# Self attention on one core: another order for VectorE's maxima and sums and for ScalarE's exponentials and copies

## The chip, the cores and the metric

The kernel runs on one core of a Trainium2 chip. The metric is the device time of one execution in microseconds (us). A core has five engines that run at the same time, each through its own list of instructions, in order: TensorE (PE in the profile; PEld is its weight loads), VectorE (DVE), ScalarE (ACT), GpSimd (POOL) and SyncE (SP). They wait for each other through semaphores only.

## The reference, cut to what matters

Three blocks with residuals over 32 batches of 128 tokens of width 128: causal self attention with 16 heads of 64, cross attention (16 heads of 8, with 128 context keys beside 128 own), and a mixture of 8 experts. The change is in the first:

```python
def self_attention(resid_stream, ...):            # called with layernorm(x): two norms in a row
    x = _layernorm(resid_stream, ln_w, ln_b)
    q = jnp.einsum('bsd,hde->bshe', x, W_q) + b_q        # k and v likewise
    scores = jnp.einsum('bqhe,bkhe->bhqk', q, k) * D_HEAD ** -0.5
    scores = jnp.where(causal, scores, -jnp.inf)
    pattern = jax.nn.softmax(scores, axis=-1)
    z = jnp.einsum('bhqk,bkhe->bqhe', pattern, v)
    return jnp.einsum('bqhe,hed->bqd', z, W_o) + b_o
x = x + self_attention(layernorm(x), ...)
```

## The kernel before

Self attention handles one batch b at a time, in four steps g = 0 to 3 (the loop over `steps`). The 16 heads of a batch are four *units* of four heads; a unit's scores (128 x 512) fill one PSUM bank. Scores for units 0 and 1 (banks 0 and 1) are one product group of TensorE in g = 0, those for units 2 and 3 (banks 2 and 3) one in g = 1. All engines run the same loop over b and g; each has its own function `self_attention` with its own order, and the order in it is written by hand. `valid(k)` says whether batch b + k exists; `back(b, parity, g, k, n)` gives the unit that was handled k steps earlier, which may be of the batch before.

For one unit the path is: scores (TensorE), `reduce_max` (VectorE, L638), four exponentials (ScalarE, L529), `reduce_sum` and `reciprocal` (VectorE, L644 and L647), multiply of the probabilities by the inverse sums (GpSimd, L388), four transposes (TensorE, L993) into bank 6, copy to `probsT` (ScalarE, L521). After unit 3 of a batch come the products with v (z, TensorE, in banks 0 and 1), two z copies (ScalarE, L539), the output product with `wo` and the residual (VectorE, L692).

Beside this run the projections for batch b + 1 (TensorE through banks 4 and 5: q in g = 0, k in g = 1, v in g = 2; VectorE copies q at L656 and k at L661, ScalarE copies v at L546), and the two norms of batch b + 2: statistics and aggregate (VectorE, L680 and L683) in g = 0 and again in g = 1, an rstd for each (GpSimd, L395 and L398), `zln` (L674) and `xn` (L686) on VectorE, the transpose of `xn` (TensorE, L950) and `xT` (VectorE, L633), which GpSimd splits in two float16 parts (L380 and L382).

TensorE's order in a batch b is:

- g = 0: scores of units 0 and 1; transposes of unit 2 of b - 1; q projection of b + 1
- g = 1: scores of units 2 and 3; transposes of unit 3 of b - 1; k projection
- g = 2: z of b - 1; transposes of unit 0 of b; v projection
- g = 3: transpose of xn of b + 2; transposes of unit 1 of b; output product of b - 1 (it waits for `sa_z_taken` and `sa_xT_taken`)

GpSimd's order is: g = 0: multiply of unit 3 of b - 1, first rstd of b + 2; g = 1: multiply of unit 0, second rstd; g = 2: multiply of unit 1; g = 3: split of xT, multiply of unit 2, bias to the residual.

In batches 30 and 31 (`run_joined`) the first steps of cross attention stand between the steps of self attention, and a last pass with b = 32 finishes batch 31. Then follow cross attention and the experts.

Of the kernel before, what the change touches and what calls it, by code (L numbers as in the profile page):

```python
# [20 lines left out]
ACT = mybir.ActivationFunctionType  # L21
AX_X = mybir.AxisListType.X

P = 128
# [5 lines left out]
G1 = 4  # L30
HPG = H // G1
E2 = D // H
HALVES = 2
# [64 lines left out]
def back(b, parity, g, k, n):  # L98

    off, unit = divmod(g - k, n)  # L100
    return off, unit, (parity + off) % 2


def build(nc, x, ctx, W_q, W_k, W_v, W_o, b_q, b_k, b_v, b_o, ln_w, ln_b, w_qkv, w_proj, b_proj,
          gate_w, gate_proj_w, up_proj_w, down_proj_w, out):
    es = ExitStack()
    with es:
        def sb(name, shape, dt=F32):
            return es.enter_context(nc.sbuf_tensor(name, shape, dt))

        def sem(name):
            return es.enter_context(nc.semaphore(name))
# [50 lines left out]
        probs = sb("probs", [P, 4, 512])  # L163
        probsT = sb("probsT", [P, 4, 512])
        zT = sb("zT", [P, PAIRS, P])
        nmax = sb("nmax", [P, 8, 4])
        rsum = sb("rsum", [P, 8, 4])
        rinv = sb("rinv", [P, 8, 4])
# [52 lines left out]
        ps = [es.enter_context(nc.psum_tensor(f"ps{i}", [P, 512], F32)) for i in range(8)]  # L221
# [28 lines left out]
        sa_scores = sem("sa_scores"); sa_max = sem("sa_max"); sa_exp = sem("sa_exp")  # L250
        sa_sums = sem("sa_sums"); sa_inverse_sums = sem("sa_inverse_sums")
# [40 lines left out]
        def bcast(ap, n):  # L292

            return ap.unsqueeze(2).to_broadcast([ap.shape[0], ap.shape[1], n])
# [208 lines left out]
        def _(act):  # L503
# [12 lines left out]
            def self_attention(b, parity, valid, steps):  # L516
                def copy_transposed(g):
                    off, u, _ = back(b, parity, g, 2, G1)
                    if valid(off):
                        act.wait_ge(sa_pT_in_bank, G1 * (b + off) + u + 1)  # L520
                        nc.scalar.copy(probsT[:, u, :], ps[6][:, :]).then_inc(sa_pT_taken, 1)  # L521

                for g in steps:
                    if g != 2:
                        copy_transposed(g)
                    if valid(0):
                        act.wait_ge(sa_max, G1 * b + g + 1)
                        for i in range(HPG):
                            last = nc.scalar.activation(probs[:, g, i * P:(i + 1) * P],  # L529
                                                        ps[g][:, i * P:(i + 1) * P], ACT.Exp,  # L530
                                                        bias=nmax[:, g, i:i + 1])
                        last.then_inc(sa_exp, 1)
                    if g == 2 and valid(-1):
                        n = b - 1
                        if valid(-2):
                            act.wait_ge(sa_output, n)
                        for half in range(HALVES):
                            act.wait_ge(sa_z_in_bank, HALVES * n + half + 1)
                            nc.scalar.copy(zT[:, 4 * half:4 * half + 4, :], ps[half][:, :]).then_inc(sa_z_taken, 1)  # L539
                    if g == 2:  # L540
                        copy_transposed(g)
                    if g == 2 and valid(1):
                        n, np_ = b + 1, (parity + 1) % 2
                        for half in range(2):
                            act.wait_ge(sa_projected, 6 * n + 5 + half)
                            nc.scalar.activation(v1[:, np_, 512 * half:512 * half + 512], ps[4 + half][:, :], ACT.Copy,  # L546
                                                 scale=1.0 / (X1_SCALE * W_SCALE)).then_inc(sa_v_taken, 1)
# [74 lines left out]
        def _(dve):  # L622
# [2 lines left out]
            dve.wait_ge(ln_ready, 1)  # L625

            def self_attention(b, parity, valid, steps):
                for g in steps:
                    if g == 3 and valid(2):
                        dve.wait_ge(sa_xT_in_bank, b + 3)  # L630
                        if valid(1):
                            dve.wait_ge(sa_x_low, b + 2)
                        nc.vector.tensor_scalar(xT[:, :], ps[7][:, 0:P], lnwb[:, 0:1], lnwb[:, 1:2],  # L633
                                                ALU.mult, ALU.add).then_inc(sa_xT_taken, 1)

                    if valid(0):
                        dve.wait_ge(sa_scores, HALVES * b + g // 2 + 1)
                        nc.vector.reduce_max(nmax[:, g, :], ps[g][:, :].rearrange("p (h k) -> p h k", h=HPG),  # L638
                                             AX_X, negate=True).then_inc(sa_max, 1)
                    off, u, _ = back(b, parity, g, 1, G1)  # L640
                    if valid(off):
                        t = G1 * (b + off) + u
                        dve.wait_ge(sa_exp, t + 1)
                        nc.vector.reduce_sum(rsum[:, u, :], probs[:, u, :].rearrange("p (h k) -> p h k", h=HPG),  # L644
                                             AX_X).then_inc(sa_sums, 1)
                        dve.wait_ge(sa_sums, t + 1)
                        nc.vector.reciprocal(rinv[:, u, :], rsum[:, u, :]).then_inc(sa_inverse_sums, 1)  # L647

                    if valid(1) and g < 2:
                        n, np_ = b + 1, (parity + 1) % 2  # L650
                        for half in range(2):
                            dve.wait_ge(sa_projected, 6 * n + 2 * g + half + 1)
                            tiles = ps[4 + half][:, :].rearrange("p (t q) -> p t q", t=4)
                            own = slice(4 * half, 4 * half + 4)
                            if g == 0:
                                last = nc.vector.scalar_tensor_tensor(  # L656
                                    out=qT[:, np_, own, :], in0=tiles,
                                    scalar=E1 ** -0.5 / (X1_SCALE * W_SCALE), in1=bcast(bq[:, own], P),
                                    op0=ALU.mult, op1=ALU.add)
                            else:  # L660
                                last = nc.vector.scalar_tensor_tensor(  # L661
                                    out=kT[:, np_, own, :], in0=tiles, scalar=1.0 / (X1_SCALE * W_SCALE),
                                    in1=bcast(bk[:, own], P), op0=ALU.mult, op1=ALU.add)
                            last.then_inc(sa_qk_taken, 1)

                    if valid(2):
                        n = b + 2
                        if g == 0:
                            if valid(-2) and not valid(-3):
                                dve.wait_ge(x_rest_loaded, 16)  # L670
                            src = x_all[:, n, :]
                        if g == 1:
                            dve.wait_ge(sa_rstd, 2 * n + 1)
                            nc.vector.tensor_scalar(zln[:, :], x_all[:, n, :], mv[:, 0, 0:1], rstd[:, 0:1],  # L674
                                                    ALU.subtract, ALU.mult).then_inc(sa_first_norm, 1)
                            dve.wait_ge(sa_first_norm, n + 1)
                            src = zln[:, :]
                        if g < 2:
                            dve.sem_inc(alone)
                            nc.vector.bn_stats(bst[:, g, :], src).then_inc(sa_stats, 1)  # L680
                            dve.wait_ge(sa_stats, 2 * n + g + 1)
                            dve.sem_inc(alone)
                            nc.vector.bn_aggr(mv[:, g, :], bst[:, g, :]).then_inc(sa_mean_var, 1)  # L683
                        if g == 2:
                            dve.wait_ge(sa_rstd, 2 * n + 2)
                            nc.vector.tensor_scalar(xn[:, :], zln[:, :], mv[:, 1, 0:1], rstd[:, 1:2],  # L686
                                                    ALU.subtract, ALU.mult).then_inc(sa_norm, 1)
                    if g == 3 and valid(-1):
                        n = b - 1
                        dve.wait_ge(sa_output, n + 1)  # L690
                        dve.wait_ge(sa_bias_added, n + 1)
                        nc.vector.tensor_tensor(x_all[:, n, :], ps[7][:, P:2 * P], x_all[:, n, :],  # L692
                                                ALU.add).then_inc(sa_residual, 1)
# [575 lines left out]
```

## Time and profile before

| | |
|---|---|
| time, three runs | median 1242.4 us (1242.32 to 1245.7) |
| profiled execution | 1243.03 us, span of the core 1241.3 us |
| TensorE busy | 1153.1 us, 93% of the span |
| VectorE busy | 943.1 us, 76% |
| ScalarE busy | 834.6 us, 67% |
| GpSimd busy | 453.6 us, 37% |
| self attention | from about 26 to 496 us of the span |

The span is what the trace shows of the core; the execution's time is a little longer. In the rows below times are in us from the start of the span; a row of a timeline is one instruction or several alike (xN), with its start and its duration, and in brackets how long the engine was idle before it and who released it. Matmul durations overlap, since matmuls are pipelined.

### The profile page before, as it was taken

How to read it: one execution, taken by the hardware profiler on the slowest of the kernel's cores; microseconds unless marked ns; L12 is line 12 of the kernel's file. 1: busy time of each engine (PE TensorE's matmuls, PEld its weight loads, DVE VectorE, ACT ScalarE, POOL GpSimd, SP SyncE). 2: the span in 40 equal slices, each digit the busy share in tenths (PEclk: the TensorE clock that was granted, in tenths of full speed). 3: DMA queues.
4: the chain of work that ended last, by engine and by line, in shares of the span. 5: the costliest groups of instructions: out<-in, count | busy, mean ns of one | idle time of the engine just before them, and what ended most of it. 6: DMA issues, size and time to landing. Idle time of an engine off the chain costs nothing.

```text
span 1241.3 us, 31536 instructions
## 1 busy us (share of the span) xinstructions
PE 1153.1 (93%) x11818; PEld 869.5 (70%) x11851; DVE 943.1 (76%) x2242; ACT 834.6 (67%) x2374; POOL 453.6 (37%) x796
## 2 busy tenths in 40 slices
PE   5889999998999997999999999999996899999997
PEld 4677777777777776777777777777774566656564
DVE  5876677776667774888888888888886778888887
ACT  2556555566555554888888888888885565555554
POOL 3544444444444443232323323233222332222222
PEclk9999999999999998999999999999998899999999
DMA  6000000000000000000000000000030000000000
GB/s 158 2 2 2 2 1 2 2 2 2 2 1 2 2 2 5 10 11 14 10 11 11 10 15 10 11 10 11 24 94 1 1 10 10 11 10 10 10 10 10
DMA packets 20666, 16.06 MB, mean 13 GB/s; under 512 B 7042, under 2 KB 18596, under 8 KB 20516
## 3 DMA queue, kind: packets, MB, share of 16 engines
q1 hardware_dynamic: 20176, 13.90, 4.1%
q8 instruction: 96, 1.57, 0.5%
q14 instruction: 54, 0.44, 0.1%
q10 hardware_dynamic: 340, 0.14, 0.1%
HBM read 11.94 MB, written 2.10 MB: 11 GB/s over the span
## 4 chain that ended last, share of the span: by engine, by line
PE 52%; issue 16%; ACT 16%; DVE 10%; POOL 6%; DMA 1%; SPq 0%; DVEq 0%; POOLq 0%
PE ps L942 38%; PE ps L1087 7%; ACT probs L564 5%; POOL h_lo L492 5%; PE ps L993 5%; DVE kT L661 3%; ACT probsT L555 3%; ACT zT L539 2%; ACT probs L529 2%; DVE nmax L638 2%; ACT probsT L521 1%; ACT k_hi L559 1%; DVE bst L680 1%; DMA wv<-in_L_attn_W_v 1%; PE ps L1120 1%
## 5 line engine op out<-in xcount | busy, mean ns | idle before, releaser
L564 ACT ACTIVATE probs<-ps,nmax 128x256 f32<-128x256 f32 x512 | 239.2, 478 | 11.2 <-DVE nmax L783 10.6
L783 DVE TENSOR_REDUCE nmax<-ps 128x2 f32<-128x512 f32 x256 | 176.3, 689 | 48.2 <-PE ps L942 45.0
L529 ACT ACTIVATE probs<-ps,nmax 128x128 f32<-128x128 f32 x512 | 148.4, 390 | 72.4 <-DVE nmax L638 72.4
L388 POOL TENSOR_TENSOR probs<-probs,rinv 128x512 f32<-128x512 f32 x128 | 133.4, 1042 | 147.2 <-DVE rinv L647 145.3
L521 ACT COPY probsT<-ps 128x512 f32<-128x512 f32 x128 | 78.4, 612 | 127.4 <-PE ps L993 127.4
L942 PE MATMUL ps<-probsT,vm 128*32 128x128 f32 x2048 | 161.5, 279 | 0.0
L555 ACT COPY probsT<-ps 128x512 f32<-128x512 f32 x224 | 131.9, 589 | 34.8 <-PE ps L1087 32.6
L1087 PE MATMUL ps<-ident,probs 128*128 128x128 f32 x1024 | 153.8, 273 | 1.2 <-ACT probs L564 1.1
L492 POOL TENSOR_TENSOR h_lo<-wk,h_hi 128x512 f16<-128x512 f32 x64 | 74.0, 1156 | 185.4 <-ACT h_hi L612 182.4
L604 ACT ACTIVATE wq<-ps 128x512 f32<-128x512 f32 x128 | 76.6, 598 | 73.2 <-PE ps L942 73.1
L1087 PEld LDWEIGHTS ps<-ident,probs 128*128 128x128 f32 x1024 | 119.6, 141 | 5.0 <-ACT probs L564 2.1
L942 PEld LDWEIGHTS ps<-probsT,vm 128*32 128x32 f32 x2048 | 92.8, 109 | 42.7 <-issue 42.6
L993 PE MATMUL ps<-ident,probs 128*128 128x128 f32 x512 | 83.6, 286 | 41.3 <-ACT probsT L521 37.1
L638 DVE TENSOR_REDUCE nmax<-ps 128x4 f32<-128x512 f32 x128 | 86.1, 672 | 38.5 <-PE ps L942 38.5
L564 ACT ACTIVATION_READ_ACCUMULATOR probs<-ps,nmax 128x1 f32 x512 | 105.8, 207 | 0.0
L612 ACT CAST h_hi<-wk 128x512 f16<-128x512 f32 x128 | 77.9, 617 | 40.9 <-DVE wk L921 40.8
L926 DVE TENSOR_TENSOR h_lo<-wk,h_hi 128x512 f16<-128x512 f32 x64 | 71.8, 1123 | 43.8 <-ACT h_hi L612 43.8
L942 PE MATMUL ps<-kT,qm 128*128 128x256 f16 x512 | 98.2, 274 | 5.7 <-ACT probs L564 5.4
L942 PE MATMUL ps<-xnT_hi,w_hi 128*128 128x512 f16 x256 | 99.6, 389 | 2.7 <-DVE wk L921 2.7
L942 PE MATMUL ps<-xnT_lo,w_hi 128*128 128x512 f16 x256 | 98.9, 386 | 0.0
L993 PEld LDWEIGHTS ps<-ident,probs 128*128 128x128 f32 x512 | 54.0, 141 | 63.8 <-POOL probs L388 50.7
L942 PE MATMUL ps<-xnT_hi,w_lo 128*128 128x512 f16 x256 | 98.6, 385 | 0.0
(194 smaller groups left out, 2872.3 us busy)
## 6 DMA issues: line engine op xcount, KB each, us to landing
ctx_row<-in_ctx SPq DMA_DIRECT2D x32, 128.0 KB, 2.0
out_x<-x_all SPq DMA_DIRECT2D x8, 256.0 KB, 2.3
kT<-in_L_ffn_down_proj_w SPq DMA_DIRECT2D x1, 1024.0 KB, 10.9
wq<-in_L_attn_W_q SPq DMA_DIRECT2D x1, 512.0 KB, 5.1
wk<-in_L_attn_W_k SPq DMA_DIRECT2D x1, 512.0 KB, 9.3
wv<-in_L_attn_W_v SPq DMA_DIRECT2D x1, 512.0 KB, 9.7
wo<-in_L_attn_W_o SPq DMA_DIRECT2D x2, 256.0 KB, 6.1
x_all<-in_x SPq DMA_DIRECT2D x1, 256.0 KB, 3.1
```

The costliest lines, as they stand in the source:

```text
L388: nc.gpsimd.tensor_tensor(pr, pr, bcast(rinv[:, u, :], P), ALU.mult).then_inc(sa_probs, 1)
L492: nc.gpsimd.tensor_tensor(h_lo[:, e % 2, 0, :], hT[:, 0, :], h_hi[:, e % 2, 0, :], ALU.subtract).then_inc(hidden_low_first, 1)
L521: nc.scalar.copy(probsT[:, u, :], ps[6][:, :]).then_inc(sa_pT_taken, 1)
L529: last = nc.scalar.activation(probs[:, g, i * P:(i + 1) * P], ps[g][:, i * P:(i + 1) * P], ACT.Exp, bias=nmax[:, g, i:i + 1])
L555: nc.scalar.copy(probsT[:, u % 4, :], ps[2 + u % 2][:, :]).then_inc(ca_pT_taken_act, 1)
L564: last = nc.scalar.activation(probs[:, g % 4, i * KEYS2:(i + 1) * KEYS2], ps[SCORE_BANKS2[g]][:, i * KEYS2:(i + 1) * KEYS2], ACT.Exp, bias ...
L612: nc.scalar.copy(h_hi[:, e % 2, i, :], hT[:, i, :]).then_inc(hidden_high, 1)
L638: nc.vector.reduce_max(nmax[:, g, :], ps[g][:, :].rearrange("p (h k) -> p h k", h=HPG), AX_X, negate=True).then_inc(sa_max, 1)
L783: nc.vector.reduce_max(nmax[:, g, 0:2], ps[SCORE_BANKS2[g]][:, :].rearrange("p (h k) -> p h k", h=2), AX_X, negate=True).then_inc(ca_max, 1)
L942: return nc.tensor.matmul(o, l, r, start=start, stop=stop, **kw)
L993: last = nc.tensor.transpose(ps[6][:, i * P:(i + 1) * P], probs[:, u, i * P:(i + 1) * P], ident[:, :])
L1087: last = nc.tensor.transpose(ps[2 + u % 2][:, i * P:(i + 1) * P], probs[:, u % 4, i * P:(i + 1) * P], ident[:, :])
```

## The change

VectorE takes the maxima of units 0 and 1 in g = 0 and does in g = 1: sum 0, maximum 2, sum 1, maximum 3. Sums 2 and 3 follow in g = 2 and 3 of the same batch (unit 3's was in g = 0 of the next). ScalarE does the exponentials of units 0 and 1 in g = 0, of unit 2 in g = 1, of unit 3 in g = 2 behind the z copies and the copy of transposed unit 0; the v copies go to g = 3, behind the copy of transposed unit 1. TensorE's, GpSimd's and SyncE's programs are unchanged, as is the number of instructions of each kind.

```diff
@@ ScalarE, self_attention @@
+                def exponentials(u):
+                    if valid(0):
+                        act.wait_ge(sa_max, G1 * b + u + 1)
+                        for i in range(HPG):
+                            last = nc.scalar.activation(probs[:, u, i * P:(i + 1) * P],
+                                                        ps[u][:, i * P:(i + 1) * P], ACT.Exp,
+                                                        bias=nmax[:, u, i:i + 1])
+                        last.then_inc(sa_exp, 1)
+
                 for g in steps:
-                    if g != 2:
-                        copy_transposed(g)
-                    if valid(0):
-                        act.wait_ge(sa_max, G1 * b + g + 1)
...
-                        last.then_inc(sa_exp, 1)
+                    if g == 0:
+                        copy_transposed(0)
+                        exponentials(0)
+                        exponentials(1)
+                    if g == 1:
+                        copy_transposed(1)
+                        exponentials(2)
                     if g == 2 and valid(-1):
...
                             nc.scalar.copy(zT[:, 4 * half:4 * half + 4, :], ps[half][:, :]).then_inc(sa_z_taken, 1)
                     if g == 2:
-                        copy_transposed(g)
-                    if g == 2 and valid(1):
+                        copy_transposed(2)
+                        exponentials(3)
+                    if g == 3:
+                        copy_transposed(3)
+                    if g == 3 and valid(1):
                         n, np_ = b + 1, (parity + 1) % 2
@@ VectorE, self_attention @@
+                def maximum(u):
+                    if valid(0):
+                        dve.wait_ge(sa_scores, HALVES * b + u // 2 + 1)
+                        nc.vector.reduce_max(nmax[:, u, :], ps[u][:, :].rearrange("p (h k) -> p h k", h=HPG),
+                                             AX_X, negate=True).then_inc(sa_max, 1)
+
+                def sums(off, u):
+                    if valid(off):
+                        t = G1 * (b + off) + u
+                        dve.wait_ge(sa_exp, t + 1)
+                        nc.vector.reduce_sum(rsum[:, u, :], probs[:, u, :].rearrange("p (h k) -> p h k", h=HPG),
+                                             AX_X).then_inc(sa_sums, 1)
+                        dve.wait_ge(sa_sums, t + 1)
+                        nc.vector.reciprocal(rinv[:, u, :], rsum[:, u, :]).then_inc(sa_inverse_sums, 1)
...
-                    if valid(0):
-                        dve.wait_ge(sa_scores, HALVES * b + g // 2 + 1)
...
-                    off, u, _ = back(b, parity, g, 1, G1)
-                    if valid(off):
...
+                    if g == 0:
+                        maximum(0)
+                        maximum(1)
+                    if g == 1:
+                        sums(0, 0)
+                        maximum(2)
+                        sums(0, 1)
+                        maximum(3)
+                    if g >= 2:
+                        sums(0, g)
```

## Rows read from the trace of the kernel before

**Rows 1.** Windows: busy us (instructions) of each engine, TensorE's clock, DMA.

```profile
53.18:455.81 402.63, 367.16 (x4296) 303.74 (x4324) 282.70 (x672) 233.66 (x672) 192.78 (x308) 1.00 0.01 2
469.71:496.41 26.70, 20.80 (x179) 17.74 (x178) 12.50 (x30) 10.77 (x28) 8.12 (x12) 0.81 0.02 6
485.00:488.00 3.00, 1.17 (x6) 0.84 (x8) 0.62 (x2) 0.22 (x2) 1.04 (x1) 0.66 0.00 0
```

**Rows 2.** Line L993 (transposes of probabilities): for whom TensorE sat idle.

```profile
  ACT probsT L521: 34.8, 29
```

**Rows 3.** Timeline of TensorE in one steady batch.

```profile
239.64 1.16 PE L942 MATMUL ps<-kT,raw_gu 64*128 64x128 f32 x16
...
242.51 0.22 PE L942 MATMUL ps<-xT_hi,w_lo 128*128 128x128 f16 x1
...
251.27 0.63 PE L993 MATMUL ps<-ident,probs 128*128 128x128 f32 x4 [1.20 <-ACT probsT L521]
...
251.74 1.95 PE L942 MATMUL ps<-wo,zT 128*128 128x128 f32 x16
...
254.05 1.16 PE L942 MATMUL ps<-kT,raw_gu 64*128 64x128 f32 x16
```

**Rows 4.** Timeline of VectorE in the same batch.

```profile
242.16 0.18 DVE L647 RECIPROCAL rinv<-rsum 128x4 f32<-128x4 f32 x1
...
242.26 1.26 DVE L656 SCALAR_TENSOR_TENSOR raw_gu<-ps,bq 128x512 f32<-128x512 f32 x2
...
243.43 0.28 DVE L680 BATCH_NORM_STATS2 bst<-x_all 128x6 f32<-128x128 f32 x1
...
243.96 0.66 DVE L638 TENSOR_REDUCE nmax<-ps 128x4 f32<-128x512 f32 x1
...
244.54 0.68 DVE L644 TENSOR_REDUCE rsum<-probs 128x4 f32<-128x512 f32 x1
...
245.25 0.18 DVE L647 RECIPROCAL rinv<-rsum 128x4 f32<-128x4 f32 x1
...
246.82 0.34 DVE L674 TENSOR_SCALAR zln<-x_all,mv,rstd 128x128 f32<-128x128 f32 x1
```

**Rows 5.** Timeline of GpSimd in the same batch: the second rstd.

```profile
248.43 0.57 POOL L398 TENSOR_TENSOR rstd<-ve,neg_half 128x1 f32<-128x1 f32 x1
```

**Rows 6.** Batch 1 by timelines, and durations (min/median/max ns) of line L686.

```profile
47.31 1.04 POOL L388 TENSOR_TENSOR probs<-probs,rinv 128x512 f32<-128x512 f32 x1
...
47.31 1.12 DVE L686 TENSOR_SCALAR xn<-zln,mv,rstd 128x128 f32<-128x128 f32 x1
...
48.49 0.33 PE L950 MATMUL ps<-ident,xn 128*128 128x128 f32 x1 [0.61 <-DVE xn L686]
...
48.86 0.41 DVE L633 TENSOR_SCALAR xT<-ps,lnwb 128x128 f32<-128x128 f32 x1 [0.42 <-PE ps L950]
...
L686 DVE TENSOR_SCALAR xn<-zln,mv,rstd x32: 315/318/1122, 9.1 to 451.3; 128x128 f32<-128x128 f32 x32
```

**Rows 7.** Timelines of batches 0 and 1: first maximum, and two waits of TensorE.

```profile
27.50 0.69 DVE L638 TENSOR_REDUCE nmax<-ps 128x4 f32<-128x512 f32 x1 [0.54 <-PE ps L942]
...
36.20 0.66 PE L993 MATMUL ps<-ident,probs 128*128 128x128 f32 x4 [0.57 <-POOL probs L388]
...
38.66 0.66 PE L993 MATMUL ps<-ident,probs 128*128 128x128 f32 x4 [0.28 <-POOL probs L388]
```

**Rows 8.** Timelines of TensorE and ScalarE at the end of self attention.

```profile
480.86 0.63 PE L993 MATMUL ps<-ident,probs 128*128 128x128 f32 x4 [1.91 <-ACT probsT L521]
...
484.62 0.58 ACT L521 COPY probsT<-ps 128x512 f32<-128x512 f32 x1 [1.47 <-PE ps L993]
...
486.83 1.11 PE L993 MATMUL ps<-ident,probs 128*128 128x128 f32 x4 [2.25 <-POOL probs L388]
...
487.87 3.68 PE L942 MATMUL ps<-probsT,v 128*64 128x128 f32 x32
...
492.24 3.78 PE L942 MATMUL ps<-wo,zT 128*128 128x128 f32 x16 [0.68 <-ACT zT L539]
```

More of the change, by code:

```diff
@@ L521, in copy_transposed @@
                         nc.scalar.copy(probsT[:, u, :], ps[6][:, :]).then_inc(sa_pT_taken, 1)
-                for g in steps:
-                    if g != 2:
-                        copy_transposed(g)
-                    if valid(0):
-                        act.wait_ge(sa_max, G1 * b + g + 1)
[L528 to L531, printed above, removed]
-                        last.then_inc(sa_exp, 1)
+                def exponentials(u):
[6 more added lines that the diff above has]
+                        last.then_inc(sa_exp, 1)
+                for g in steps:
+                    if g == 0:
[5 more added lines that the diff above has]
+                        exponentials(2)
                     if g == 2 and valid(-1):
@@ L634, in self_attention @@
                                                 ALU.mult, ALU.add).then_inc(sa_xT_taken, 1)
-                    if valid(0):
-                        dve.wait_ge(sa_scores, HALVES * b + g // 2 + 1)
-                        nc.vector.reduce_max(nmax[:, g, :], ps[g][:, :].rearrange("p (h k) -> p h k", h=HPG),
-                                             AX_X, negate=True).then_inc(sa_max, 1)
-                    off, u, _ = back(b, parity, g, 1, G1)
-                    if valid(off):
[L642 to L647, printed above, removed]
+                    if g == 0:
[8 more added lines that the diff above has]
+                        sums(0, g)
                     if valid(1) and g < 2:
```

## The prediction

> **What bounds the kernel now.** I read the stages first. Self attention runs in a steady rhythm from 53.18 to 455.81 us, with TensorE busy 367 of 403 us at full clock; after 469.71 comes the end of self attention, where TensorE is busy only 20.8 of 26.7 us and its clock falls: 0.66 granted in 485 to 488 us [rows 1]. The waits of the transposes of self-attention probabilities then show one kind of stall: 34.8 us in 29 times, 1.20 us each, for ScalarE's copy of transposed probabilities [rows 2]. So the most that this stage can give is 29 x 1.2 = 35 us.
>
> The timeline of TensorE shows where it stands. A batch takes 254.05 - 239.64 = 14.41 us from score product to score product, and the only gap is before the transposes of unit 1 at 251.27, with 1.20 us idle [rows 3]. On VectorE the same batch runs almost without a pause from the q copies to the first norm, and the maximum of unit 2 comes only after it [rows 4]; behind that maximum ScalarE does exponentials, two z copies and the copy that TensorE waits for. The change takes that queue apart. The question is what is late next.
>
> **The change, part by part.** Instruction counts do not change: 4 maxima, 4 sums, 4 x 4 exponentials and the copies stay. Only order changes.
>
> *ScalarE.* The exponentials of unit 1 follow those of unit 0, unit 2's come at g = 1 and unit 3's behind the z copies. The copy of unit 0's transposes is no longer behind a late maximum: it can end some 1.2 us sooner. The v copies move from g = 2 to g = 3, behind the copy of unit 1; they would end near 253.7, and the next q projection that needs the banks starts near 255.7, so that costs nothing (if that cover of 2 us went, its shortfall would be paid in every batch).
>
> *VectorE, and through it GpSimd.* In g = 0 and 1 VectorE now runs four maxima and two sums before the second norm of the batch; before, two maxima and two sums, one of them left over from the batch behind. The k copies, zln and the second mean and variance stand behind them. GpSimd's order is unchanged: it must compute the second rstd *before* it multiplies unit 1's probabilities by their inverse sums, and TensorE's transposes of unit 1 need that product. So the wait that the change removes on ScalarE is replaced by one on VectorE and GpSimd. I sum that chain from the last q product, since the second q copy can't begin before it. Steps from the start of one instruction to the start of the next [rows 4, 5]:
>
> - last q product ends 242.51 + 0.22 = 242.73 [rows 3]; 0.05 to VectorE (estimate; a crossing of engines takes 0.06 in [rows 6])
> - second q copy to first statistics 0.585 (half of 243.43 - 242.26); statistics and aggregate 0.53 (to 243.96)
> - sum 0 to reciprocal 0.71 (244.54 to 245.25); reciprocal to maximum 2 0.10 (242.16 to 242.26)
> - maximum 2, sum 1, to reciprocal 1.29 (243.96 to 245.25); 0.10; maximum 3 0.58 (243.96 to 244.54)
> - k copies 1.17, as the q copies (in the rows the k pair is stretched by waiting for its products, which it won't now)
> - zln to the end of the second rstd: 246.82 to 248.43 + 0.57 = 249.00, so 2.18
>
> Together 0.05 + 7.25 = 7.30, so rstd is ready at R = 250.03, against 249.00 before. If only the multiply of 1.04 followed, TensorE could transpose at 251.13, and 0.14 us of the 1.20 would be won. But xn (VectorE) waits for the same rstd. Before, it starts after its reciprocal, when rstd is long there, and takes 0.32. Now it starts together with GpSimd's multiply. One batch of the kernel before has this meeting: batch 1, where both start at 47.31; xn takes 1.12 us, and ends 0.08 after the multiply [rows 6]. Of 32 xn it is the only long one (median 0.318). TensorE's transpose of xn stands *before* the transposes of unit 1 in its queue, and the output product waits for xT. From batch 1: multiply R to R + 1.04; xn ends + 0.08; transpose starts + 0.06 (48.49); xT starts + 0.37 (48.86) and takes 0.41; + 0.06 to the output product: R + 2.02 = 252.05. It started at 251.74 [rows 3]. So a steady batch becomes 0.31 us *longer*, rounded to 0.30: 28 batches (2 to 29) x 0.30 = **+8.4 us**.
>
> The Trainium skill (SBUF — State Buffer, Who interferes with whom) has a rule for this meeting: a VectorE tensor_scalar in a two-port mode and a GpSimd instruction exclude each other for a whole instruction, and the one issued first wins. The trace agrees (1.12 against 0.318). By that rule the other order is possible as well; it is a rival below.
>
> *First batches.* In batch 0 there is no leftover sum to lose. The added maximum moves the q copies: 27.50 + 0.61 + 0.58 + 1.17 = 29.86 for the first statistics, and 6.66 of the sum above gives R = 36.52. The multiply ends at 37.56, xn 37.64, and unit 1's transposes, behind xn's, start at 37.8 in place of 36.20: + 1.6. In batch 1 the transposes of unit 2 already wait for GpSimd (0.28 idle) [rows 7], whose multiply now stands behind a later xT: + 0.3 (estimate: 0 to 0.6), and batch 1's own lengthening is about 0.2. Together **+ 2.1** (1.4 to 2.7).
>
> *End of self attention.* Batch 30 has no norm of its own: the chain there is shorter, unit 1 is multiplied about 0.6 sooner than the copy allowed. In batch 31 there are no projections to cover the wait: unit 1's transposes wait 1.91 us until 480.86, for the same ScalarE queue [rows 8]. With maxima 2 and 3 drawn forward this queue is shorter. Followed through the same steps they start near 479.0: 1.85 sooner in all. Last, unit 3's transposes of batch 31 wait 2.25 us, until 486.83, for a multiply whose sum stood on VectorE behind the residual and cross attention's preparations. Now the sum stands in g = 3 before the residual. Late next is the copy of unit 2's transposes, which ends 484.62 + 0.58 = 485.20; + 0.06 gives 485.26, 1.57 sooner. With those gaps gone TensorE is idle at most about 1 us at a time, less than the 1.2 us in each steady batch, at which the clock stayed at 1.00. So I take it that the clock stays at 2.4 GHz through z and output. At 1.2 GHz they took 1.11, 3.68 and 3.78 us [rows 8]; the output product takes 1.95 at 2.4 GHz [rows 3], and by that ratio the three save about 0.5 + 1.8 + 1.8 = 4.1, less 0.2 for z's new wait. Sum 1.85 + 1.57 + 3.9 = **- 7.3** (6.3 to 8.0 if the clock holds).
>
> Cross attention and the experts are not touched.
>
> **Sum.** 8.4 + 2.1 - 7.3 = + 3.2 us. The profiled execution had a span of 1241.3 and took 1243.03, 0.6 above the median of 1242.4. So 1244.5 span, 1246.2 for a profiled run, and **1245.6 us** as median. A measurement of this kernel tells about 0.3%, 3.7 us, from no change.
>
> **Rivals.**
> 1. *The clock falls at the end all the same.* For: it fell after a 2.25 us gap, and gaps of about 1 remain. Against: the steady stage. Then 3.7 of the 7.3 are not won: 1249.3, slower.
> 2. *Xn and the multiply don't meet, or don't hinder each other.* Then xT is early and only the multiply counts: 28 x - 0.15, start + 1.4, end - 7.3, so 1232, faster. Against: batch 1. It decides if the multiply starts over 0.3 us after xn.
> 3. *Xn gets through first.* The multiply is then late by 0.32, the transposes start at R + 1.46 and the output product 0.47 later: 251.96, + 0.22 a batch, 1243.3.
> 4. *VectorE's chain is longer than its parts*: the sums of g = 1 run beside GpSimd's multiply of unit 0. If that cost each batch 0.2 more, 5.6 us: 1251.2, slower. Against: in the rows sums take 0.68 whatever runs beside them.
> 5. *The gain comes whole*: 28 x 1.2 + 7 gives 1202. Only if GpSimd's second rstd did not stand before unit 1's multiply, which the program's order excludes.
>
> **How the numbers follow.** Forecast 0.45, rival 1 0.18, rival 2 0.11, rival 3 0.08, rival 4 0.13, rival 5 0.03, others 0.02. The forecast's own range is 1242.3 to 1248.9 (28 x 0.1, and the two edges). It and rivals 1, 3 and most of 4 lie in 1238 to 1251.5; what is left out is rivals 2 and 5 and part of 4. The forecast stands just inside the bound of 3.7 us, so its chance is split, 0.27 within and 0.18 above. Faster: 0.14 from rivals 2 and 5, and 0.03 of the rest; within: 0.27 + 0.08 + 0.04; slower: 0.18 + 0.18 + 0.08 by clock, size and chain.
>
> **What would show it.** In the changed profile: a period of about 14.7 us; xn's median near 1.1 us and its start beside the multiply; TensorE idle before xn's transpose (1.4 us) and not for the copy; VectorE's k copies 1.1 us later against the scores; the last z products at half their former duration. The prediction is wrong if xn stays at 0.32, if TensorE's wait is again for ScalarE, or if the clock row still shows a fall before cross attention.

## The result, and the profile after

| | before | changed |
|---|---|---|
| median | 1242.4 us (1240.56 to 1246.26, 5 runs) | 1252.51 us (1251.56 to 1254.57, 5 runs) |
| profiled execution | 1243.03 us, span 1241.3 | 1254.57 us, span 1252.9 |
| VectorE, ScalarE busy | 943.1, 834.6 us | 966.0, 845.7 us |

The ratio is 1.0077, 95% interval 1.0054 to 1.0100: slower by 10.1 us, where + 3.2 was forecast. The profiled executions differ by 11.5 us, since the one of the changed kernel was the slowest of its five runs. In the changed kernel's line numbers xn is L709, the transposes L1016, the transpose of xn L973, xT L658, and products L965.

Where the time went can be read from four marks on VectorE: the first maximum of batch 0, of batch 2 and of batch 30, and the last residual. This is its timeline in the changed kernel:

```profile
29.32 1.29 DVE L641 TENSOR_REDUCE nmax<-ps 128x4 f32<-128x512 f32 x2 [0.54 <-PE ps L965]
...
58.62 1.29 DVE L641 TENSOR_REDUCE nmax<-ps 128x4 f32<-128x512 f32 x2 [1.24 <-PE ps L965]
...
475.94 1.29 DVE L641 TENSOR_REDUCE nmax<-ps 128x4 f32<-128x512 f32 x2 [1.31 <-PE ps L965]
...
507.34 0.29 DVE L715 TENSOR_TENSOR x_all<-ps,x_all 128x128 f32<-128x128 f32 x1 [5.89 <-PE ps L965]
```

And in the kernel before:

```profile
53.18 0.69 DVE L638 TENSOR_REDUCE nmax<-ps 128x4 f32<-128x512 f32 x1 [1.24 <-PE ps L942]
...
457.39 0.69 DVE L638 TENSOR_REDUCE nmax<-ps 128x4 f32<-128x512 f32 x1 [1.31 <-PE ps L942]
...
496.06 0.29 DVE L692 TENSOR_TENSOR x_all<-ps,x_all 128x128 f32<-128x128 f32 x1 [10.40 <-PE ps L942]
```

With 27.50 for the first of them [rows 7] the stages compare so (us; spans of one profiled execution each):

| stage | before | changed | difference | forecast |
|---|---|---|---|---|
| up to batch 0 | 27.50 | 29.32 | + 1.8 | 0 |
| batches 0 and 1 | 25.68 | 29.30 | + 3.6 | + 2.1 |
| batches 2 to 29 | 404.21 | 417.32 | + 13.1 | + 8.4 |
| batch 30 to the last residual | 38.67 | 31.40 | - 7.3 | - 7.3 |
| the rest | 745.2 | 745.6 | + 0.3 | 0 |

One steady batch of the changed kernel, VectorE from the first statistics to xT:

```profile
300.40 0.28 DVE L703 BATCH_NORM_STATS2 bst<-x_all 128x6 f32<-128x128 f32 x1
...
303.67 1.28 DVE L684 SCALAR_TENSOR_TENSOR kT<-ps,bk 128x512 f32<-128x512 f32 x2
304.87 0.34 DVE L697 TENSOR_SCALAR zln<-x_all,mv,rstd 128x128 f32<-128x128 f32 x1
...
307.08 1.05 DVE L709 TENSOR_SCALAR xn<-zln,mv,rstd 128x128 f32<-128x128 f32 x1 [0.33 <-POOL rstd L398]
308.55 0.41 DVE L658 TENSOR_SCALAR xT<-ps,lnwb 128x128 f32<-128x128 f32 x1 [0.42 <-PE ps L973]
```

GpSimd in the same batch:

```profile
306.47 0.57 POOL L398 TENSOR_TENSOR rstd<-ve,neg_half 128x1 f32<-128x1 f32 x1
307.01 1.04 POOL L388 TENSOR_TENSOR probs<-probs,rinv 128x512 f32<-128x512 f32 x1
```

TensorE:

```profile
308.19 0.33 PE L973 MATMUL ps<-ident,xn 128*128 128x128 f32 x1 [1.21 <-DVE xn L709]
308.35 0.60 PE L1016 MATMUL ps<-ident,probs 128*128 128x128 f32 x4
309.11 2.02 PE L965 MATMUL ps<-wo,zT 128*128 128x128 f32 x16 [0.16 <-DVE xT L658]
311.49 1.16 PE L965 MATMUL ps<-kT,raw_gu 64*128 64x128 f32 x16
```

These rows show the meeting that before had in batch 1 alone [rows 6]; in the changed kernel 30 of the 32 xn are long: the multiply at 307.01, xn at 307.08 with 1.05 us in place of 0.32, and TensorE idle 1.21 us for xn, then 0.16 for xT. ScalarE's copy no longer keeps anyone: the wait of [rows 3] has gone, and another of the same size stands in its place. ScalarE's queue is ready early:

```profile
305.72 0.59 ACT L521 COPY probsT<-ps 128x512 f32<-128x512 f32 x1
```

This copy ends at 306.31, and TensorE's last products ahead of xn's transpose end at 306.98, so TensorE would not have waited for it. The period, from one residual to the next, is 14.84 us (residuals at 459.50 and 474.34; 14.83 by the aggregates), against 14.41.

TensorE's clock fell at other places than before. Windows of the changed kernel (the granted clock is the third number from the end; 0.50 is 1.2 GHz):

```profile
24.00:28.00 4.00, 3.87 (x17) 3.50 (x18) 2.18 (x14) 0.00 (x0) 0.59 (x2) 0.59 0.11 37
42.00:44.00 2.00, 2.00 (x17) 1.71 (x14) 1.29 (x2) 0.44 (x1) 1.70 (x3) 0.50 0.04 8
294.00:296.00 2.00, 1.78 (x9) 1.55 (x9) 0.29 (x1) 0.14 (x1) 1.94 (x3) 0.50 0.00 0
485.00:505.00 20.00, 17.34 (x182) 14.78 (x183) 13.43 (x29) 12.56 (x33) 10.78 (x17) 1.00 0.03 8
```

The engine had been idle 2.31 us for xn before the fall in batch 1, and 1.54 us before that of 294. But behind a wait of 1.55 us in the same kernel the clock stayed up (1.00 in 54 to 62 us):

```profile
39.51 0.33 PE L973 MATMUL ps<-ident,xn 128*128 128x128 f32 x1 [2.31 <-DVE xn L709]
...
54.10 0.33 PE L973 MATMUL ps<-ident,xn 128*128 128x128 f32 x1 [1.55 <-DVE xn L709]
...
291.76 0.33 PE L973 MATMUL ps<-ident,xn 128*128 128x128 f32 x1 [1.54 <-DVE xn L709]
```

At the end of self attention the clock stays at 2.4 GHz; z and output product are at their full pace:

```profile
502.60 1.97 PE L965 MATMUL ps<-probsT,v 128*64 128x128 f32 x32
505.25 2.05 PE L965 MATMUL ps<-wo,zT 128*128 128x128 f32 x16 [0.69 <-ACT zT L546]
```

### The profile page after: what moved, and what is told of

It reads as the page before. It is cut to its first block, busy times and chain, and to the rows that moved or that the text cites. A ratio compares the mean times of both kernels' runs of the same rounds, so it can differ in the third digit from the quotient of the medians.

```text
span 1252.9 us, 31536 instructions
## 1 busy us (share of the span) xinstructions
PE 1159.1 (93%) x11818; PEld 869.7 (69%) x11851; DVE 966.0 (77%) x2242; ACT 845.7 (68%) x2374; POOL 449.5 (36%) x796
## 3 DMA queue, kind: packets, MB, share of 16 engines
q8 instruction: 96, 1.57, 0.5%
## 4 chain that ended last, share of the span: by engine, by line
PE 40%; DVE 23%; issue 17%; ACT 10%; POOL 7%; DMA 1%; SPq 0%; DVEq 0%; POOLq 0%
PE ps L965 30%; PE ps L1110 7%; DVE nmax L641 6%; ACT probs L574 5%; POOL h_lo L492 5%; DVE kT L684 3%; DVE rsum L648 3%; ACT probsT L565 3%; DVE xn L709 3%; DVE raw_gu L679 2%; POOL rstd L398 1%; DVE bst L703 1%; ACT k_hi L569 1%; DVE xT L658 1%; DVE mv L706 1%
## 5 line engine op out<-in xcount | busy, mean ns | idle before, releaser
L521 ACT COPY probsT<-ps 128x512 f32<-128x512 f32 x128 | 75.1, 587 | 164.7 <-PE ps L1016 164.7
L965 PE MATMUL ps<-probsT,vm 128*32 128x128 f32 x2048 | 161.5, 279 | 0.0
L565 ACT COPY probsT<-ps 128x512 f32<-128x512 f32 x224 | 132.1, 590 | 34.7 <-PE ps L1110 32.5
L1110 PE MATMUL ps<-ident,probs 128*128 128x128 f32 x1024 | 153.8, 273 | 1.2 <-ACT probs L574 1.1
L527 ACT ACTIVATE probs<-ps,nmax 128x128 f32<-128x128 f32 x512 | 143.2, 383 | 9.9 <-DVE nmax L641 9.9
L1110 PEld LDWEIGHTS ps<-ident,probs 128*128 128x128 f32 x1024 | 119.6, 141 | 5.0 <-ACT probs L574 2.1
L965 PEld LDWEIGHTS ps<-probsT,vm 128*32 128x32 f32 x2048 | 92.8, 109 | 42.7 <-issue 42.6
L641 DVE TENSOR_REDUCE nmax<-ps 128x4 f32<-128x512 f32 x128 | 83.5, 673 | 39.2 <-PE ps L965 39.2
L965 PE MATMUL ps<-kT,qm 128*128 128x256 f16 x512 | 98.2, 274 | 5.8 <-ACT probs L574 5.4
L965 PE MATMUL ps<-xnT_hi,w_hi 128*128 128x512 f16 x256 | 99.0, 387 | 2.7 <-DVE wk L944 2.7
L965 PE MATMUL ps<-xnT_lo,w_hi 128*128 128x512 f16 x256 | 98.5, 385 | 0.0
L965 PE MATMUL ps<-xnT_hi,w_lo 128*128 128x512 f16 x256 | 98.3, 384 | 0.0
L965 PE MATMUL ps<-xT_hi,w_hi 128*128 128x128 f16 x512 | 91.7, 222 | 3.6 <-POOL xT_lo L382 2.0
L395 POOL TENSOR_SCALAR ve<-mv 128x1 f32<-128x1 f32 x64 | 14.3, 223 | 216.8 <-DVE mv L706 216.8
```

What stands on the lines that cost most here:

```text
L527: last = nc.scalar.activation(probs[:, u, i * P:(i + 1) * P], ps[u][:, i * P:(i + 1) * P], ACT.Exp, bias=nmax[:, u, i:i + 1])
L565: nc.scalar.copy(probsT[:, u % 4, :], ps[2 + u % 2][:, :]).then_inc(ca_pT_taken_act, 1)
L641: nc.vector.reduce_max(nmax[:, u, :], ps[u][:, :].rearrange("p (h k) -> p h k", h=HPG), AX_X, negate=True).then_inc(sa_max, 1)
L965: return nc.tensor.matmul(o, l, r, start=start, stop=stop, **kw)
L1110: last = nc.tensor.transpose(ps[2 + u % 2][:, i * P:(i + 1) * P], probs[:, u % 4, i * P:(i + 1) * P], ident[:, :])
```

## The experiments

Each is set against the kernel before in runs on the same chip; the interval is that of the ratio.

### 1. The multiply of unit 1 ahead of the second rstd

```diff
@@ the changed kernel, GpSimd, self_attention @@
-                    off, u, _ = back(b, parity, g, 1, G1)
-                    if valid(off):
+                    for off, u in {0: ((-1, 3),), 1: ((0, 0), (0, 1)), 2: (), 3: ((0, 2),)}[g]:
+                        if not valid(off):
+                            continue
```

> The changed kernel, with GpSimd's multiply of unit 1 ahead of the second rstd instead of behind it. Theory 1 (GpSimd's order turns the longer VectorE queue into TensorE's wait: the multiply starts together with xn, xn takes 1.05 us and the transposes of both come late): xn back at 0.32 us, output product 0.7 us earlier in a batch, period 14.1 us against 14.83, and no fall of the clock; about 1228 us. Theory 2 (the longer VectorE queue ahead of the second rstd is the cost by itself, whoever multiplies when): period at best 14.7, 1249 us or more.

Measured: 1228.21 us (1227.48 to 1228.84), ratio 0.9887 (0.9870 to 0.9903). TensorE's timeline:

```profile
349.24 0.33 PE L974 MATMUL ps<-ident,xn 128*128 128x128 f32 x1 [0.49 <-DVE xn L710]
349.40 0.60 PE L1017 MATMUL ps<-ident,probs 128*128 128x128 f32 x4
350.16 2.02 PE L966 MATMUL ps<-wo,zT 128*128 128x128 f32 x16 [0.16 <-DVE xT L659]
```

VectorE's xn now has no neighbour on GpSimd:

```profile
348.84 0.34 DVE L710 TENSOR_SCALAR xn<-zln,mv,rstd 128x128 f32<-128x128 f32 x1 [0.33 <-POOL rstd L399]
```

The period is 14.12 us (residuals at 338.10 and 352.22), 0.71 less than in the changed kernel. VectorE's queue is as long as there (6.68 us from the first statistics to xn in both), so theory 2 falls: most of the cost was in what GpSimd did behind that queue. The idle 0.49 us that remains before xn's transpose is the queue itself. One part of the expectation failed: the clock did fall, once, before batch 0 (0.66 in 24 to 29 us).

### 2. Xn first, then the multiply

```diff
@@ the changed kernel, GpSimd, before the multiply @@
                         pool.wait_ge(sa_inverse_sums, t + 1)
+                        if g == 2 and valid(2):
+                            pool.wait_ge(sa_norm, b + 3)
```

> The changed kernel, with GpSimd's multiply of unit 1 made to wait until xn is written, so that the two never run together. Theory 1: xn takes 0.32 us, the multiply starts about 0.4 us later than now, and the transposes of unit 1 are what the output product follows: period 14.69 us, about 1248 us. Theory 2 (the stretch of xn from 0.32 to 1.05 us is all that lengthens the batch): period about 14.1 us, 1231 us.

Measured: 1251.25 us (1248.08 to 1252.39), ratio 1.0075 (1.0056 to 1.0095). TensorE's timeline:

```profile
345.98 0.33 PE L975 MATMUL ps<-ident,xn 128*128 128x128 f32 x1 [0.50 <-DVE xn L711]
347.16 0.66 PE L1018 MATMUL ps<-ident,probs 128*128 128x128 f32 x4 [0.86 <-POOL probs L390]
347.66 1.95 PE L967 MATMUL ps<-wo,zT 128*128 128x128 f32 x16
```

Xn takes 0.35 us and the wait has only moved: 0.50 for xn, 0.86 for the multiply. The period is 14.80 us, 0.03 below the changed kernel's and 0.11 above my figure. Theory 2 falls: keeping the two apart by making one wait gives next to nothing. The price is that they don't run side by side, not which one loses.

### 3. Zln in PSUM

```diff
@@ the changed kernel, VectorE, self_attention @@
-                            nc.vector.tensor_scalar(zln[:, :], x_all[:, n, :], mv[:, 0, 0:1], rstd[:, 0:1],
+                            nc.vector.tensor_scalar(ps[7][:, 2 * P:3 * P], x_all[:, n, :], mv[:, 0, 0:1], rstd[:, 0:1],
...
-                            src = zln[:, :]
+                            src = ps[7][:, 2 * P:3 * P]
...
-                            nc.vector.tensor_scalar(xn[:, :], zln[:, :], mv[:, 1, 0:1], rstd[:, 1:2],
+                            nc.vector.tensor_scalar(xn[:, :], ps[7][:, 2 * P:3 * P], mv[:, 1, 0:1], rstd[:, 1:2],
```

> The changed kernel with zln kept in PSUM (bank 7) instead of SBUF, so that xn reads PSUM; order and waits unchanged, and xn and the multiply still start together. Theory 1 (the two exclude each other by their access to SBUF): xn about 0.4 us, multiply 1.04 us, side by side; the output product 0.54 us earlier, period 14.25 us, 1236 to 1239 us. Theory 2 (the meeting costs nothing, only the multiply's place behind the second rstd does): period 14.8 us, 1252 us.

Measured: 1236.06 us (1234.6 to 1238.04), ratio 0.9945 (0.9925 to 0.9966). GpSimd, VectorE and TensorE:

```profile
339.79 1.04 POOL L388 TENSOR_TENSOR probs<-probs,rinv 128x512 f32<-128x512 f32 x1
...
339.86 0.41 DVE L709 TENSOR_SCALAR xn<-ps,mv,rstd 128x128 f32<-128x128 f32 x1 [0.33 <-POOL rstd L398]
...
340.89 0.66 PE L1016 MATMUL ps<-ident,probs 128*128 128x128 f32 x4 [0.23 <-POOL probs L388]
```

The two start as before, 0.07 us apart, but xn ends after 0.41 us, beside the multiply. The period is 14.31 us (residuals at 443.59 and 457.90). So without the meeting over SBUF a batch is 0.52 us shorter, and the change would have been a gain of 6.7 us (against 1242.79 on that chip). It is not the whole 0.64 us that xn gained, since the transposes of unit 1 now wait 0.23 us for the multiply. No semaphore makes xn wait for the multiply, in the changed kernel either: these two engines hold each other without one, which the description of the cores ahead left out. The clock still fell before batch 0 and in batch 1 here (0.57 in 40 to 44 us), behind a wait of 1.74 us. By the Trainium skill's page SBUF — State Buffer (Who interferes with whom) VectorE and GpSimd share one pair of ports, which a tensor_scalar can take in its two-port modes; a VectorE instruction outside these modes, with at most one input in SBUF, does not contend. The trace agrees: 1.05 us from SBUF, 0.41 from PSUM.

### 4. The maximum of unit 3 behind the second norm

```diff
@@ the changed kernel, VectorE, self_attention @@
                     if g == 1:
                         sums(0, 0)
                         maximum(2)
                         sums(0, 1)
-                        maximum(3)
...
                             nc.vector.bn_aggr(mv[:, g, :], bst[:, g, :]).then_inc(sa_mean_var, 1)
+                    if g == 1:
+                        maximum(3)
+                    if valid(2):
+                        n = b + 2
```

> The changed kernel with VectorE's maximum of unit 3 behind the second norm's aggregate instead of ahead of the k copies. Theory 1 (TensorE's wait is the sum of VectorE's queue ahead of the second rstd): the batch is shorter by one maximum, 0.58 us, period 14.25 us, 1236 us. Theory 2 (something else, as ScalarE's exponentials of unit 3, is late next): less than 0.3 us a batch, above 1244 us.

Measured: 1232.72 us (1232.21 to 1233.24), ratio 0.9918 (0.9900 to 0.9935). The period is 14.23 us (residuals at 437.96 and 452.19), 0.60 less for one maximum of 0.58: VectorE's queue ahead of the second rstd counts one for one. It came out 3 us better than 1236: the fall of the clock in batch 1 and that near 294 have gone as well. Yet TensorE waits for xn in batch 1 as long as in the changed kernel, so the length of that wait does not decide by itself whether the clock falls:

```profile
37.33 0.33 PE L976 MATMUL ps<-ident,xn 128*128 128x128 f32 x1 [2.31 <-DVE xn L712]
...
37.00:45.00 8.00, 7.14 (x90) 5.95 (x91) 6.04 (x14) 4.94 (x14) 4.63 (x9) 1.00 0.01 2
```

Xn still meets the multiply (0.86 us).

### 5. Both mends

Experiments 1 and 4 together.

> The multiply of unit 1 ahead of the second rstd, and the maximum of unit 3 behind the second aggregate. Theory 1: the two shortenings add, since xn's path and not the multiply's sets the output product once the multiply is early: period 13.6 us, where TensorE has next to no gap left, 1214 us. Theory 2 (TensorE's own work or another wait is reached before): 14.0 us, 1225 us.

Measured: 1216.42 us (1215.58 to 1217.18), ratio 0.9786 (0.9769 to 0.9804): 26.4 us faster than the kernel before. TensorE's timeline and its window over the steady stage:

```profile
338.38 0.33 PE L977 MATMUL ps<-ident,xn 128*128 128x128 f32 x1
338.54 0.60 PE L1020 MATMUL ps<-ident,probs 128*128 128x128 f32 x4
339.31 2.02 PE L969 MATMUL ps<-wo,zT 128*128 128x128 f32 x16 [0.16 <-DVE xT L659]
```

```profile
60.00:430.00 370.00, 363.65 (x4189) 293.90 (x4187) 271.43 (x649) 234.15 (x649) 182.46 (x298) 1.00 0.01 2
```

The period is 13.69 us, 0.1 above the expected one; in a steady batch TensorE waits for nothing longer than the 0.16 us for xT, and it is busy 98%. The gap that ScalarE's queue caused before, and GpSimd's after the change, is closed.

### 6. The new order at the end only

The kernel before for batches 0 to 29; both engines' changed functions for 30 and 31, and the sum of unit 3 of batch 29 at the start of 30.

```diff
+            def self_attention(b, parity, valid, steps):
+                f = self_attention_after if b >= NB - 2 else self_attention_before
+                f(b, parity, valid, steps)
```

> The kernel before for batches 0 to 29, the changed order from batch 30 on. Theory 1 (the changed order wins 7.3 us at the end of self attention, by shorter waits and a clock that stays up, and loses everywhere else): 1235 us. Theory 2 (the win at the end depends on what came before, or is chance of the clock): 1242 us.

Measured: 1236.16 us (1235.78 to 1237.76), ratio 0.9953 (0.9936 to 0.9970), a gain of 6.3 us. From the first maximum of batch 30 (457.79) to the last residual (489.24) it takes 31.45 us, 7.2 less than the 38.67 of before, and the clock doesn't fall there (1.00 in 478 to 496 us). The gain at the end stands by itself.

### 7. ScalarE's part alone

The new ScalarE order in batches 0 to 29, with VectorE's as before (the last two batches keep ScalarE's old order, since the new one would wait there for a maximum that waits for ScalarE).

```diff
+            def self_attention(b, parity, valid, steps):
+                f = self_attention_before if b >= NB - 2 else self_attention_after
+                f(b, parity, valid, steps)
```

> The kernel before, with ScalarE's new order in batches 0 to 29 and VectorE's order as before. Theory 1 (the wait before unit 1's transposes starts at VectorE's late maximum 2, ScalarE's order is no part of it): the same stall of 1.20 us, 1242 us. Theory 2 (ScalarE's queue is the bottleneck by its own order): up to 1.2 us a batch shorter, 1209 us.

Measured: 1241.31 us (1239.49 to 1243.73), ratio 0.9989 (0.9977 to 1.0001). No difference is shown. The same stall stands in TensorE's timeline, and ScalarE sits idle for VectorE's late maximum ahead of the exponentials that stand before its copy:

```profile
349.11 1.14 ACT L560 ACTIVATE probs<-ps,nmax 128x128 f32<-128x128 f32 x4 [2.26 <-DVE nmax L685]
...
351.85 0.63 PE L1040 MATMUL ps<-ident,probs 128*128 128x128 f32 x4 [1.21 <-ACT probsT L554]
```

This run tells something of the end as well. Its last two batches run the programs of before, but the clock was low for less long: 0.53 in 486 to 489 us and 1.00 from 490, against 0.50 in 486 to 496 us of before. The stage from batch 30 to the last residual took 36.36 us (456.78 to 493.14) in place of 38.67.

### 8. VectorE's part alone

ScalarE's function of the kernel before in the changed kernel.

```diff
@@ the changed kernel, ScalarE, self_attention @@
-                    if g == 0:
-                        copy_transposed(0)
-                        exponentials(0)
-                        exponentials(1)
...
+                    if g != 2:
+                        copy_transposed(g)
+                    if valid(0):
+                        act.wait_ge(sa_max, G1 * b + g + 1)
```

> VectorE's new order with ScalarE's order as before. Theory 1 (VectorE's queue ahead of the second rstd sets the batch, so what stretches it shows one for one): sum 1 must now wait for exponentials that ScalarE does only behind the copy of unit 3's transposes, some 1.26 us later, and the period goes from 14.83 to about 16.1 us, 1285 us. Theory 2 (ScalarE's order has slack enough to hide it): 1252 us.

Measured: 1321.59 us (1319.2 to 1322.57), ratio 1.0625 (1.0602 to 1.0648). Sum 1 on VectorE waits as forecast:

```profile
340.22 0.69 DVE L638 TENSOR_REDUCE rsum<-probs 128x4 f32<-128x512 f32 x1 [1.20 <-ACT probs L529]
```

TensorE's timeline and a window show what I had not counted:

```profile
346.14 0.48 PE L963 MATMUL ps<-ident,xn 128*128 128x128 f32 x1 [2.32 <-DVE xn L699]
...
347.26 2.94 PE L955 MATMUL ps<-wo,zT 128*128 128x128 f32 x16
```

```profile
345.00:349.00 4.00, 2.86 (x13) 2.75 (x14) 1.46 (x2) 1.50 (x5) 2.66 (x4) 0.60 0.02 4
```

TensorE now waits 2.31 us before xn's transpose in every batch from 2 to 29. In 21 of these 28 the clock is at 1.2 GHz for a while around the end of that wait, and the output product, as here, takes 2.94 us in place of 2.02. In the other 7, with the same wait, it stays up:

```profile
363.37 0.33 PE L963 MATMUL ps<-ident,xn 128*128 128x128 f32 x1 [2.31 <-DVE xn L699]
...
362.00:367.00 5.00, 3.47 (x27) 2.83 (x29) 2.52 (x5) 1.63 (x5) 3.52 (x7) 1.00 0.00 2
```

Between residuals a batch with the fall takes 17.2 to 17.4 us and one without 16.42, against 14.83. So the longer chain costs 1.6 us and the clock another 0.8 to 1.0 where it falls. Both theories named too little, though the first has the direction and the place.

### 9. The changed kernel again

> The changed kernel once more, to see which parts of its excess come back. Theory 1 (the falls of TensorE's clock before batch 0, in batch 1 and once in the steady stage come from the longer gaps before xn's transpose, and recur in number if not in place): 1252.5 us, the period 14.83 us again, and again a fall or more before 500 us. Theory 2 (they were chance of one execution): no fall, about 1248 us.

Measured: 1254.09 us (1253.08 to 1255.23), ratio 1.0087 (1.0064 to 1.0109). Its windows, in another execution than the one shown above:

```profile
24.00:28.00 4.00, 3.48 (x17) 3.36 (x17) 2.56 (x12) 0.00 (x0) 0.98 (x2) 0.57 0.15 37
42.00:44.00 2.00, 2.00 (x16) 1.72 (x15) 0.79 (x2) 0.53 (x2) 2.00 (x3) 0.50 0.00 0
292.00:298.00 6.00, 5.42 (x35) 4.32 (x37) 1.83 (x5) 1.57 (x3) 3.40 (x6) 0.72 0.01 3
```

The falls came back at all three places, in both profiled executions that there are of this kernel.

## Why the prediction was right or wrong

**Right: where the wait went.** The wait for ScalarE came from VectorE's late maximum (experiment 7: with ScalarE's order alone ScalarE is idle 2.26 us for that maximum, and TensorE 1.21 us for the copy); the change turned it into a wait for xn, behind VectorE's longer queue and GpSimd's second rstd (experiments 1 and 4). The sum from the first statistics to the end of rstd was 6.66 us; the rows give 307.04 - 300.40 = 6.64. That xn meets the multiply in every batch was read from one long xn of 32. The changed kernel has 30 long ones, and experiment 3 shows that their length goes with a source in SBUF.

**Right: the end.** - 7.3 was forecast and measured, with the clock held, and the three terms fit one by one: measured against the start of batch 30, unit 1's transposes in batch 31 start 1.9 us sooner (forecast 1.85), unit 3's another 1.45 (1.57), and what follows them takes 3.9 less (3.9). Experiment 6 has it alone, with 6.3 of it in the median. That the last term fits so well is in part luck: it rests on how long the clock stayed low in one execution of before, and experiment 7, with the same programs there, lost 2.3 us less to it.

**Wrong: + 3.2 where + 10.1 was measured, outside the range.** Two terms of the sum failed, and a stage that I had put at nothing. In the profiled executions the difference is 11.5, so 8.3 more than forecast: 3.4 from the period of a steady batch, 1.3 from the rest of the steady stage, 1.5 from batches 0 and 1, 1.8 ahead of batch 0, and 0.3 behind self attention, where nothing was changed.

- *A steady batch, 0.30.* It is 0.42, so 28 x 0.12 = 3.4 us. The step is the end of the chain from batch 1: I gave 0.06 us from the end of xT to the output product, as for the transpose of xn. It is 309.11 - 308.96 = 0.15; the steps ahead of it give 0.04 back, so that from rstd to the output product it is 2.07 us for 2.02. And an output product that starts behind an idle TensorE takes 2.02 us, where one that follows the transposes at once takes 1.95 ([rows 3]; experiments 2 and 3 have 1.95 as well, experiment 1 has 2.02). In batch 1 of before TensorE waited for ScalarE's copy behind xT, which hid both.
- *The clock.* I asked of the clock only whether it stays up at the end. The step that failed was to cost longer gaps of TensorE elsewhere by their own length. The first batches gave + 3.6 for + 2.1, and the steady stage 1.3 beyond the 11.8 of its period; in both the clock was at 1.2 GHz for a while behind a wait for xn of 2.31 and 1.54 us. (The second is the one steady batch in which sum 0 came late, 0.20 us idle for an exponential at 284.46, so that the usual 1.21 us grew by 0.33; that part is no cost of the clock.) Experiment 2's kernel, whose gaps are cut in two, ran the first two batches without a fall: 27.70 us (26.76 to 54.46), 2.0 above before, near the forecast. What makes the clock fall behind one such wait and not behind another of the same length (experiments 4 and 8) stays open.
- *Ahead of batch 0, a term put at nothing.* Of the 1.8 us 0.3 are there before the fall: TensorE's products at 16.65 (16.36 in before) wait for VectorE's q copies, which follow the landing of a weight load. That moves between executions of the same kernel (17.35 in experiment 9), so it is no effect of the change. The rest goes with the fall (TensorE's 16 products of the bias took 3.57 us for 2.05). Why it comes there, where the change moves little, no run settles. Of the eight profiled executions with VectorE's new order from batch 0 on seven have it (experiment 2 does not), and of the three with the old order none (before, experiments 6 and 7).

The rivals: 1 (the clock falls) happened, but at other places than I looked; 2 and 5 did not; 3 did not come by itself (the multiply went first and xn took 1.05 us in each steady batch), and built as experiment 2 it differs by 0.03 us a batch from the forecast's order; 4 fell, since the sums beside the multiply took 0.68 as ever.

## What to carry to other kernels

When a reordering shortens one engine's queue, sum the other queues from the last common point, and follow the result through an engine whose order did not change: here GpSimd's rstd ahead of a multiply decided, and turning the two round is worth 24 us. Look at the longest case of a group (min/median/max), not its mean: one xn of 1.12 us among 32 of 0.32 held the price of the change. Where a wait grows beyond those that the clock has so far survived, give a range: its length alone, and its length with the work behind it at half the clock. Waits of 2.31 us brought the fall in most batches here, not in all.

## What the runs showed of the hardware

- An f32 tensor_scalar from SBUF on VectorE (0.32 us alone) that starts 0.07 us after a GpSimd tensor_tensor of 1.04 us ends 0.08 us after it, at 1.05 us; started 0.26 us after one (experiment 4) it takes 0.86 us and ends 0.08 us after it again. From PSUM it takes 0.41 us in the same place. A sum of 128x512 beside the same multiply keeps its 0.68 us (302.29 in the changed kernel).
- The length of TensorE's wait did not decide alone whether the granted clock fell. In the changed kernel it fell behind waits of 2.31 us (batch 1) and 1.54 us (0.50 in 294 to 296 us) and stayed up behind one of 1.55 us (54.10) and those of 1.2 us; the places came back in a second execution (42 to 44 and 292 to 298 us). In experiment 4 it stayed up behind 2.31 us, and in experiment 8, with 2.31 us in each steady batch, it fell in 21 of 28.
